# Attention probabilities transposed in 32 by 32 blocks on VectorE and moved across partitions by DMA, in place of TensorE transposes

## Chip, cores and metric

The kernel runs on one core of a Trainium2 chip. The metric is the device time of one execution in microseconds, of which the median over the timed runs counts.

## What is computed

Two transformer layers over 8 batches of 112 tokens of width 1024. Each layer is a cross attention to 375 context rows and a small mixture of low rank experts, with a layer norm ahead of each. The change touches the attention of the second layer, which the reference computes so (32 query heads in 8 groups of 4, each group with one key and value head, head width 128):

```
q = (query @ wq).reshape(bs, sq, HQ, DK).transpose(0, 2, 1, 3)
k = (key @ wk).reshape(bs, sk, HKV, DK)        # repeated for the 4 heads of a group
v = (value @ wv).reshape(bs, sk, HKV, DV)
q = apply_rope(q, pos)
k = apply_rope(k, curr_seq_pos + jnp.arange(sk))
scores = jnp.einsum('bhqd,bhkd->bhqk', q, k) / scale
attn = jax.nn.softmax(scores + m[:, None, :, :], axis=-1)
out = jnp.einsum('bhqk,bhkd->bhqd', attn, v)
return out.transpose(0, 2, 1, 3).reshape(bs, sq, HQ * DV) @ wo
```

## The kernel before

Every float32 product is made of three TensorE passes over operands that are split into a high and a low part (`split_product`, line 204: high x high, high x low, low x high). The high part is a copy on ScalarE (ACT) into a rounded type, the low part a subtraction on VectorE (DVE) or GpSimd (POOL).

The first layer, the key and value projections and the query projection (`query1_phase`) come first. The attention then runs as 64 **steps** (`attention_phase`), one for each group g of 4 heads and each batch u, with s = 8g + u. The steps are written out one by one on each engine. The order on an engine is the order of its instructions, engines wait for each other by semaphores, and all DMAs are issued from one queue, SP's. In step s:

- TensorE makes the scores of step s+1 (4 heads, 12 matmuls of 376 columns), the transposes of the probabilities of step s (line 1780, 12 of them: 4 heads by 3 tiles of 128 keys, through the identity into three PSUM banks), 24 matmuls of 448 columns, and the output of step s (9 matmuls of 448 columns: v by transposed probabilities). The 24 are the output projection of an earlier quad of batches (`project`); in the first four steps (`FILLED`) they are the last of the query projection.
- VectorE adds the mask to the scores and takes their maximum (line 1515), negates it (1519), later scales the exponentials by the inverse sum (1535), makes the low parts of the transposed probabilities (1722) and of the output (1736), and adds up the projection (1713).
- ScalarE takes the exponentials (1526), copies the high parts of the transposed probabilities out of PSUM (1659), and makes the high parts of q (1476), k (1478), v, the output and the output weights.
- GpSimd makes the low parts of q, k (both line 1491), v (1496) and the output weights (1683).
- SP loads q, k and v of later steps (lines 1460, 1463, 1468), in half of the steps a tile of output weights (1617), and in the first steps stores the last rotated queries.

The score tile `e_scores` has the queries in partitions and the keys in the row, so the probabilities must be transposed before they can meet v, whose keys are in partitions.

Of the kernel before, what the change touches and what calls it, by code (L numbers as in the profile page):

```python
# [14 lines left out]
ALU = mybir.AluOpType  # L15
# [21 lines left out]
LOWEST = -3.4028234663852886e38  # L37
# [69 lines left out]
class LoraSems:  # L107
    def __init__(self, sem, name):
        self.mid = sem(f"{name}_mid")
        self.chain = sem(f"{name}_chain")  # L110
        self.gate_exp = sem(f"{name}_gexp")
# [98 lines left out]
def build(nc, x, ctx_nat, ctx_t, mask, wq0_t, wk0, bq, bk, a0, b0, wq1, wk1, wv1, wo1, a1, b1,  # L210
# [5 lines left out]
    with ExitStack() as outer:  # L216
# [16 lines left out]
        with ExitStack() as heads, ExitStack() as layer0:  # L233
# [5 lines left out]
            with ExitStack() as context, nc.Block() as block:  # L239
# [11 lines left out]
                last_heads = query1_phase(nc, k, first, q1, layer0, block)  # L251
                layer0.close()
                attention_phase(nc, k, first, last_heads, heads, block)
# [570 lines left out]
def layer0_phase(nc, k, keys, chunks, q1, ctx, block):  # L824
# [36 lines left out]
    sn, sl = NormSems(sem, "ln23"), LoraSems(sem, "lora0")  # L861
# [349 lines left out]
def query1_phase(nc, k, first, q1, buffers, block):  # L1211
# [3 lines left out]
    sb, _, _ = buffers_of(nc, buffers)  # L1215
    sem = k.sem
    bank = k.banks[4:8]
    rope = sb("q_rope", [P, 2, SEQ])
    straight, crossed = sb("q_straight", [P, 2, HALF]), sb("q_crossed", [P, 2, HALF])
# [20 lines left out]
    def _(sp):  # L1240
# [22 lines left out]
        with sp.Fori(1, LAST - 2) as i:  # L1263
# [6 lines left out]
        load_w(LAST - 2, 0)  # L1270
        first.load(sp)
        for t in range(2):
            if t == 1:
                load_w(LAST - 2, 1)
            for h in range(2):
                store(4 * (LAST - 2) + 2 * t + h, LAST - 2, t, h)
        load_w(LAST - 1, 0)
        first.load_next(sp)
        for t in range(2):
            if t == 1:  # L1280
                load_w(LAST - 1, 1)
            for h in range(2):
                store(4 * (LAST - 1) + 2 * t + h, LAST - 1, t, h)
# [7 lines left out]
    def _(act):  # L1291
# [10 lines left out]
        with act.Fori(2, LAST - 1) as i:  # L1302
            for t in range(2):
                weight_high(i, t, 4 * i + 2 * t + 2)
        weight_high(LAST - 1, 0, 4 * LAST - 2)
        first.split_high(act)
        weight_high(LAST - 1, 1, 4 * LAST)
        weight_high(LAST, 0, 4 * LAST + 2)
        first.exps(act, 0, 0, range(PER_GROUP))
# [3 lines left out]
    def _(pool):  # L1313
# [5 lines left out]
        with pool.Fori(1, LAST - 1) as i:  # L1319
            for t in range(2):  # L1320
                weight_low(i, t)
        weight_low(LAST - 1, 0)
        first.split_low(pool)
        weight_low(LAST - 1, 1)
        weight_low(LAST, 0)
        weight_low(LAST, 1)
# [21 lines left out]
    def _(dve):  # L1348
# [7 lines left out]
        with dve.Fori(1, LAST - 1) as i:  # L1356
# [3 lines left out]
        unit = 4 * (LAST - 1)  # L1360
        first.take_mask(dve)
        rotated_half(dve, unit, LAST - 1, 0, 0)
        first.mask_scores(dve, 0, 0, (0, 1))
        rotated_half(dve, unit + 1, LAST - 1, 0, 1)
        first.mask_scores(dve, 0, 0, (2, 3))
        rotated_half(dve, unit + 2, LAST - 1, 1, 0)
        first.normalise(dve, 0, 0)
        rotated_half(dve, unit + 3, LAST - 1, 1, 1)
# [10 lines left out]
    def _(pe):  # L1379
# [12 lines left out]
        with pe.Fori(1, LAST - 1) as i:  # L1392
# [3 lines left out]
        unit = 4 * (LAST - 1)  # L1396
        half_tile(unit, LAST - 1, 0, 0)
        first.scores(pe, 0, 0, (0, 1))
        half_tile(unit + 1, LAST - 1, 0, 1)
        first.scores(pe, 0, 0, (2, 3))  # L1400
        half_tile(unit + 2, LAST - 1, 1, 0)
        half_tile(unit + 3, LAST - 1, 1, 1)
# [17 lines left out]
class AttentionSteps:  # L1420
# [5 lines left out]
    def __init__(self, nc, ctx, k):  # L1426
        sb, pair, sem = buffers_of(nc, ctx, "right")
        self.k = k
        self.s_bank = k.banks[0:2]
        H = PER_GROUP  # L1430
        self.raw_q, self.raw_k = sb("e_raw_q", [P, 2, H, SEQ]), sb("e_raw_k", [P, 2, KEYS_EVEN])
        self.raw_v = sb("e_raw_v", [P, 2, KEY_TILES, P])
        self.q, self.kt = pair("e_q", [P, 2, H, SEQ]), pair("e_k", [P, 2, KEYS_EVEN])
# [611 lines left out]
```

## Time and profile before

| | |
|---|---|
| median of 3 runs | 1875.65 us (1875.37 to 1876.58) |
| profiled execution, its own time | 1872.77 us |
| its span, first to last instruction | 1870.7 us |
| busy: PE, DVE, ACT, POOL | 98%, 58%, 34%, 33% of the span |
| mean granted TensorE clock | 0.998 of full speed |
| attention steps: first transposes of step 0 to those of step 63 | 1149.1 to 1781.5 us of the span |

The span is cut into stages with different limits, so shares over the whole say little about the attention alone. A matmul's row shows a duration that overlaps with the next one's. What one costs is the distance between starts.

### The profile page before, as it was taken

The numbers are of one execution on the slowest core, as the hardware profiler recorded it, in microseconds if no ns is written. First come the engines' busy times: TensorE is split into PE (matmuls) and PEld (weight loads), VectorE is DVE, ScalarE is ACT, GpSimd is POOL, SyncE is SP. The second block draws the span as 40 slices with busy tenths as digits, with TensorE's granted clock in tenths as the row PEclk, the third lists the DMA queues.
The fourth block names the chain that finished last, engine by engine and source line by source line (L and its number), as shares of the span: only waits on it lengthen the run. The fifth ranks groups of instructions, "written<-read, shape, count | busy, mean of one in ns | idle before, by whom it ended". The sixth has DMA issues, their size and how long they took to land.

```text
span 1870.7 us, 27823 instructions
## 1 busy us (share of the span) xinstructions
PE 1829.2 (98%) x9628; PEld 1643.6 (88%) x9628; DVE 1091.2 (58%) x2481; ACT 636.2 (34%) x1345; POOL 610.1 (33%) x427
## 2 busy tenths in 40 slices
PE   6999999999999999999999999999999999999997
PEld 5999899999777777778999999899999999999985
DVE  5631275657222222126666668877777777777766
ACT  4211210102222222222111013666656666665612
POOL 2323531226222222202222233444435444353413
PEclk9999999999999999999999999999999999999999
DMA  4112342344533333314223234332323323232223
GB/s 125 57 56 78 131 130 80 101 137 147 169 121 120 116 118 108 110 61 132 96 93 105 100 117 128 107 97 79 103 76 99 92 79 108 78 92 85 59 74 108
DMA packets 138317, 190.40 MB, mean 102 GB/s; under 512 B 42672, under 2 KB 109360, under 8 KB 137328
## 3 DMA queue, kind: packets, MB, share of 16 engines
q1 hardware_dynamic: 138224, 189.21, 32.3%
q8 instruction: 52, 0.85, 0.2%
q14 instruction: 41, 0.34, 0.1%
HBM read 142.25 MB, written 46.92 MB: 101 GB/s over the span
## 4 chain that ended last, share of the span: by engine, by line
PE 83%; DVE 3%; issue 1%; DMA 1%; POOL 1%; ACT 0%; SPq 0%; DVEq 0%; POOLq 0%; ACTq 0%
PE bank L204 74%; PE bank L1780 4%; PE bank L1167 2%; PE bank L184 1%; PE bank L197 1%; PE bank L101 1%; DVE e_scores L1535 1%; DMA aw_weights_then_ctx_rows<-in_wk 1%; DVE e_scores L1515 0%; POOL w_rest_low L756 0%; DVE e_p_t_low L1722 0%; PE bank L1152 0%; DVE e_mask_then_layer_ffn L77 0%; DVE q_rotated_then_x_rows L1929 0%; DVE e_mask_then_layer_ffn L92 0%
## 5 line engine op out<-in xcount | busy, mean ns | idle before, releaser
L204 PE MATMUL bank<-shared_operand_high,w_first_high 128*128 128x448 f32 (+1 forms) x768 | 280.2, 365 | 6.2 <-POOL w_first_low L491 2.7
L204 PE MATMUL bank<-shared_operand_low,w_first_high 128*128 128x448 f32 (+1 forms) x768 | 279.4, 364 | 0.0
L204 PE MATMUL bank<-shared_operand_high,w_first_low 128*128 128x448 f32 (+1 forms) x768 | 279.3, 364 | 0.0
L1526 ACT ACTIVATE e_scores<-e_scores,e_nmax 112x375 f32<-112x375 f32 x256 | 155.5, 615 | 120.2 <-DVE e_nmax L1519 114.7
L317 POOL TENSOR_TENSOR shared_operand_low<-ctx_raw,shared_operand_high 128x768 fp32r<-128x768 f32 x64 | 118.4, 1863 | 204.0 <-ACT shared_operand_high L313 204.0
L204 PEld LDWEIGHTS bank<-shared_operand_high,w_first_high 128*128 128x128 f32 x768 | 145.3, 189 | 18.8 <-POOL w_first_low L491 3.0
L204 PEld LDWEIGHTS bank<-shared_operand_high,w_first_low 128*128 128x128 f32 x768 | 145.2, 189 | 11.7
L204 PEld LDWEIGHTS bank<-shared_operand_low,w_first_high 128*128 128x128 f32 x768 | 145.2, 189 | 11.2
L1515 DVE CUSTOM_DVE_ANT_0 e_scores<-bank,e_mask_then_layer_ffn 112x375 f32<-112x375 f32 x256 | 139.8, 546 | 9.2 <-PE bank L1780 0.4
L1316 POOL TENSOR_TENSOR w_first_low<-aw_weights_then_ctx_rows,w_first_high 128x1024 fp32r<-128x1024 f32 x30 | 71.7, 2391 | 224.4 <-ACT w_first_high L1298 224.4
L1496 POOL TENSOR_TENSOR e_v_low<-e_raw_v,e_v_high 128x384 fp32r<-128x384 f32 x64 | 65.2, 1019 | 226.6 <-ACT e_v_high L1485 226.6
L204 PE MATMUL bank<-shared_operand_high,w_rest_high 128*128 128x376 f32 x384 | 128.8, 335 | 2.7 <-POOL w_rest_low L756 2.7
L204 PE MATMUL bank<-shared_operand_low,w_rest_high 128*128 128x376 f32 x384 | 128.6, 335 | 0.0
L204 PE MATMUL bank<-shared_operand_high,w_rest_low 128*128 128x376 f32 x384 | 128.6, 335 | 0.0
L313 ACT ACTIVATE shared_operand_high<-ctx_raw 128x768 fp32r<-128x768 f32 x64 | 52.8, 842 | 210.6 <-DMA ctx_raw<-in_ctx_t 192.4
L1713 DVE TENSOR_TENSOR y_t<-bank,y_t 128x448 f32<-128x448 f32 x112 | 70.0, 625 | 87.0 <-PE bank L204 85.3
L1298 ACT ACTIVATE w_first_high<-aw_weights_then_ctx_rows 128x1024 fp32r<-128x1024 f32 x30 | 31.8, 1061 | 253.1 <-PE bank L204 240.2
L204 PE MATMUL bank<-w_rest_high,shared_operand_high 128*128 128x512 f32 x288 | 112.9, 392 | 0.0
L204 PE MATMUL bank<-w_rest_high,shared_operand_low 128*128 128x512 f32 x288 | 112.5, 391 | 0.0
L204 PE MATMUL bank<-w_rest_low,shared_operand_high 128*128 128x512 f32 x288 | 112.2, 389 | 0.0
L1722 DVE TENSOR_TENSOR e_p_t_low<-bank,e_p_t_high 128x448 fp32r<-128x448 f32 x192 | 107.6, 616 | 5.8 <-ACT e_p_t_high L1659 5.8
L1535 DVE TENSOR_SCALAR e_scores<-e_scores,e_inv 112x375 f32<-112x375 f32 x256 | 96.9, 437 | 2.2
(243 smaller groups left out, 4404.3 us busy)
## 6 DMA issues: line engine op xcount, KB each, us to landing
ctx_raw<-in_ctx_t SPq DMA_DIRECT2D x64, 384.0 KB, 3.7
e_raw_wo<-in_wo SPq DMA_DIRECT2D x32, 512.0 KB, 4.9
aw_weights_then_ctx_rows<-in_wq SPq DMA_DIRECT2D x30, 512.0 KB, 3.5
q_rotated<-q_rotated_then_x_rows SPq DMA_DIRECT2D x64, 224.0 KB, 1.9
e_raw_q<-q_rotated SPq DMA_DIRECT2D x64, 224.0 KB, 2.8
v_rows<-v_out SPq DMA_DIRECT2D x48, 256.0 KB, 2.1
e_raw_v<-v_rows SPq DMA_DIRECT2D x64, 192.0 KB, 3.4
k_rotated<-k_rotated_sb SPq DMA_DIRECT2D x64, 188.0 KB, 1.9
```

Source lines behind the costliest of these rows:

```text
L204: mm = pe.matmul(out, stationary[a], moving[b], start=(first and i == 0), stop=(last and i == 2))
L313: act.activation(k.ctx_ring[0][slot][:, 2 * j:2 * j + 2, :], k.c_raw[:, j % 2], ACT.Copy).then_inc(done, 1)
L317: pool.tensor_tensor(k.ctx_ring[1][slot][:, 2 * j:2 * j + 2, :], k.c_raw[:, j % 2], f32(k.ctx_ring[0][slot][:, 2 * j:2 * j + 2, :]), ALU.s ...
L1167: mm = pe.matmul(row_banks[h][0:SEQ, :], et[:, kt, :], cn[:, kt, h * 512:(h + 1) * 512], start=(kt == 0), stop=(kt == KEY_TILES - 1))
L1316: pool.tensor_tensor(k.w_first[1][:, t], k.raw[:, t], f32(k.w_first[0][:, t]), ALU.subtract).then_inc(w_low, 1)
L1496: pool.tensor_tensor(self.v[1][:, t], self.raw_v[:, t], f32(self.v[0][:, t]), ALU.subtract).then_inc(self.v_low, 1)
L1515: dve.tensor_tensor_reduce(self.s_buf[:, t, h, 0:KEYS], self.s_bank[h % 2][0:SEQ, 0:KEYS], self.mask[:, u, :], 1.0, LOWEST, ALU.add, ALU.m ...
L1526: act.activation(self.s_buf[:, t, h, 0:KEYS], self.s_buf[:, t, h, 0:KEYS], ACT.Exp, bias=self.nm[:, t, h:h + 1], accum_out=self.total[:, t ...
L1535: dve.tensor_scalar(self.s_buf[:, t, h, 0:KEYS], self.s_buf[:, t, h, 0:KEYS], self.inv[:, t, h:h + 1], None, ALU.mult).then_inc(self.norme ...
L1713: dve.tensor_tensor(k.yt[:, tile, at:at + HALF], y_bank[t][:, 0:HALF], k.yt[:, tile, at:at + HALF], ALU.add).then_inc(y_added, 1)
L1722: dve.tensor_tensor(pt[1][:, c, :], p_bank[c][:, 0:HALF], f32(pt[0][:, c, :]), ALU.subtract).then_inc(pt_low, 1)
L1780: mm = pe.transpose(p_bank[c][:, h * SEQ:(h + 1) * SEQ], s_buf[:, t, h, c * P:(c + 1) * P], k.ident[0:SEQ, 0:SEQ])
```

## The change

The queries of a batch, 112, are laid out as 4 blocks of 28 in 4 times 32 partitions, the spare places being zero, so that the scores fill 128 partitions. VectorE transposes the probabilities of two heads by one instruction (32 by 32 blocks, each within its 32 partitions), twice a step. The blocks of one query block then lie in the wrong partitions for three quarters of the keys. SP issues 16 DMAs a step, from 32 partitions of one SBUF tile to 32 partitions of another, 384 floats in each, which bring them together (`shuffle`). The 12 TensorE transposes of a step and their PSUM banks are gone. So are the 4 negations: the query rotation carries a minus sign, the mask is negated once, VectorE takes the minimum, and the exponential is taken with scale -1.

Scores are made three steps ahead of their use, normalised and transposed two steps ahead. ScalarE normalises two of the four heads, GpSimd makes two of the three low parts of the probabilities, now from SBUF instead of PSUM. The scores have four banks, the output two.

```diff
     def scores(self, pe, s, u, heads):
...
-            split_product(pe, self.s_bank[h % 2][0:SEQ, 0:KEYS_EVEN], [x[:, t, h, :] for x in self.q],
+            split_product(pe, self.s_bank[h][:, 0:KEYS_EVEN],
+                          [x[:, t, h].rearrange("p i b -> p (i b)") for x in self.q],
                           [x[:, t, :] for x in self.kt], True, True).then_inc(self.scored, 1)
...
+    def normalise_last(self, act, s, u):
+        t = u % 2
+        act.wait_ge(self.inverted, s + 1)
+        for h in (2, 3):
+            act.activation(self.s_buf[:, t, h, 0:KEYS], self.s_buf[:, t, h, 0:KEYS], ACT.Copy,
+                           scale=self.inv[:, t, h:h + 1]).then_inc(self.last_normed, 1)
+
+    def transpose(self, dve, s, u, heads):
...
+        dve.transpose(self.in_blocks[:, t, :, h * piece:(h + 2) * piece].rearrange("p j (m k) -> p m j k", k=BLOCK),
+                      self.s_buf[:, t, h:h + 2, :].rearrange("p h (c j k) -> p (h c) j k", j=BLOCKS, k=BLOCK)
+                      ).then_inc(self.transposed, 1)
+
+    def shuffle(self, sp, s):
...
+        sp.wait_ge(self.transposed, 2 * s + 2)
+        if s >= 2:
+            sp.wait_ge(self.pt_low_first, s - 1)
+            sp.wait_ge(self.pt_low, 2 * s - 2)
+        for i in range(BLOCKS):
+            for j in range(BLOCKS):
+                sp.dma_start(self.pt_raw[t][BLOCK * j:BLOCK * (j + 1), i],
+                             self.in_blocks[BLOCK * i:BLOCK * (i + 1), t, j]).then_inc(self.shuffled[t], 16)
...
         def step(s, u, g):
...
-            for c in range(KEY_TILES):
-                if s >= 1:
-                    pe.wait_ge(pt_low, 3 * s - 3 + c + 1)
-                elif c == 2:
-                    pe.wait_ge(last_heads.read, last_heads.units + 1)
-                for h in range(H):
-                    mm = pe.transpose(p_bank[c][:, h * SEQ:(h + 1) * SEQ],
-                                      s_buf[:, t, h, c * P:(c + 1) * P],
-                                      k.ident[0:SEQ, 0:SEQ])
-                mm.then_inc(turned, 1)
+            if s + AHEAD < STEPS:
+                first.scores(pe, s + AHEAD, u + AHEAD, range(H))
```

On SP's queue a middle step with a tile of output weights holds these rows before (q, k, v, output weights):

```order
L1460 DMA e_raw_q<-q_rotated 128x4x112
L1463 DMA e_raw_k<-k_rotated 128x376
L1468 DMA e_raw_v<-v_rows 128x3x128
L1617 DMA e_raw_wo<-in_wo 128x4x256
L1460 DMA e_raw_q<-q_rotated 128x4x112
```

and these now, where `e_shuffled` and `e_shuffled_then_xn_t` are the two targets of the shuffle and `q_rotated_then_x_rows` holds the transposed blocks:

```order
L1639 DMA e_shuffled_then_xn_t<-q_rotated_then_x_rows 32x384 x16
L1516 DMA e_raw_then_a<-q_rotated 128x4x112
L1519 DMA e_raw_then_a<-k_rotated 128x376
L1524 DMA e_raw_then_a<-v_rows 128x3x128
L1735 DMA e_raw_wo<-in_wo 128x4x256
L1639 DMA e_shuffled<-q_rotated_then_x_rows 32x384 x16
```

Four DMAs a step became twenty; the sixteen stand behind the step's loads and ahead of the next step's.

On VectorE a middle step before, from the mask of the first head (ISA rows of line 1515 are the masking and its accumulator read):

```order
L1515 ISA e_scores,e_max<-bank,e_mask_then_layer_ffn 112x375
L1519 TENSOR_SCALAR e_nmax<-e_max 112x1
L1722 TENSOR_TENSOR e_p_t_low<-bank,e_p_t_high 128x448 x3
L1713 TENSOR_TENSOR y_t<-bank,y_t 128x448
...
L1532 RECIPROCAL e_inv<-e_total 112x4
L1535 TENSOR_SCALAR e_scores<-e_scores,e_inv 112x375 x4
L1736 TENSOR_TENSOR e_o_t_first_low<-bank,e_o_t_first_high 128x4x112
```

and a whole step now, the accumulator reads left out:

```order
L1597 RECIPROCAL e_inv<-e_total 128x4
L1603 TENSOR_SCALAR e_scores<-e_scores,e_inv 128x375
L1840 TENSOR_TENSOR e_o_t_second_low<-bank,e_o_t_second_high 128x4x4x28
L1582 ISA e_scores,e_least<-bank,e_mask_then_layer_ffn 128x375
...
L1603 TENSOR_SCALAR e_scores<-e_scores,e_inv 128x375
...
L1625 STREAM_TRANSPOSE q_rotated_then_x_rows<-e_scores 128x6x4x32
L1859 TENSOR_TENSOR e_p_t_low<-e_shuffled,e_p_t_high 128x448
...
L1625 STREAM_TRANSPOSE q_rotated_then_x_rows<-e_scores 128x6x4x32
...
L1834 TENSOR_TENSOR y_t<-bank,y_t 128x448 x2
```

Two transposes came in, spread between the masks. One low part and two scalings are left, and both additions of the projection stand at the end of the step.

## Rows read from the trace of the kernel before

**Rows 1.** The page, part 1: busy us, share of the span, instructions.

```profile
PE 1829.2 (98%) x9628; PEld 1643.6 (88%) x9628; DVE 1091.2 (58%) x2481; ACT 636.2 (34%) x1345; POOL 610.1 (33%) x427
```

**Rows 2.** The chain that ended last, 1400 to 1500 us: start, us, what.

```profile
1412.89 1.15 PE bank L1780 x12
1414.05 8.81 PE bank L204 x45
```

**Rows 3.** Busy time by stretch: us; PE, PEld, DVE, ACT, POOL; clock; DMA share; GB/s.

```profile
1149.10:1781.50 632.40, 629.04 (x3598) 589.14 (x3596) 502.42 (x1460) 394.86 (x977) 274.19 (x220) 1.00 0.32 91
1412.73:1422.70 9.97, 9.97 (x59) 9.37 (x58) 7.85 (x24) 6.66 (x17) 5.50 (x4) 1.00 0.44 117
1442.00:1452.00 10.00, 10.00 (x59) 9.41 (x58) 7.77 (x24) 5.87 (x16) 3.13 (x3) 1.00 0.22 63
```

**Rows 4.** Groups by line: out<-in, shapes, count; busy us, mean ns; idle before.

```profile
L1722 DVE TENSOR_TENSOR e_p_t_low<-bank,e_p_t_high 128x448 fp32r<-128x448 f32 x192 | 107.6, 616 | 5.8 <-ACT e_p_t_high L1659 5.8
L1491 POOL TENSOR_TENSOR e_q_low<-e_raw_q,e_q_high 128x448 fp32r<-128x448 f32 x64 | 74.9, 1170 | 56.7 <-ACT e_q_high L1476 56.7
```

**Rows 5.** Timeline of PE, then of PEld: start, us, instruction.

```profile
300.00 0.33 PE L204 MATMUL bank<-shared_operand_high,w_first_high 128*128 128x376 f32 x1
300.17 0.34 PE L204 MATMUL bank<-shared_operand_low,w_first_high 128*128 128x376 f32 x1
...
300.00 0.19 PEld L204 LDWEIGHTS bank<-shared_operand_low,w_first_high 128*128 128x128 f32 x1
```

**Rows 6.** Timeline of DVE in one step.

```profile
1450.61 1.45 DVE L1535 TENSOR_SCALAR e_scores<-e_scores,e_inv 112x375 f32<-112x375 f32 x4
...
1453.39 0.15 DVE L1519 TENSOR_SCALAR e_nmax<-e_max 112x1 f32<-112x1 f32 x1
1453.58 0.55 DVE L1515 CUSTOM_DVE_ANT_0 e_scores<-bank,e_mask_then_layer_ffn 112x375 f32<-112x375 f32 x1
...
1454.24 1.68 DVE L1722 TENSOR_TENSOR e_p_t_low<-bank,e_p_t_high 128x448 fp32r<-128x448 f32 x3
```

**Rows 7.** Timeline of ACT in one step.

```profile
1442.65 0.51 ACT L1478 ACTIVATE e_k_high<-e_raw_k 128x376 fp32r<-128x376 f32 x1
...
1444.44 0.62 ACT L1526 ACTIVATE e_scores<-e_scores,e_nmax 112x375 f32<-112x375 f32 x1
...
1445.04 0.62 ACT L1526 ACTIVATE e_scores<-e_scores,e_nmax 112x375 f32<-112x375 f32 x1
```

**Rows 8.** Timeline of SP's queue in one step: start and us of each issue.

```profile
1401.12 0.37 SPq L1468 DMA_DIRECT2D e_raw_v<-v_rows  x1
1401.54 0.55 SPq L1617 DMA_DIRECT2D e_raw_wo<-in_wo  x1
1408.02 0.37 SPq L1460 DMA_DIRECT2D e_raw_q<-q_rotated  x1
1408.43 0.51 SPq L1463 DMA_DIRECT2D e_raw_k<-k_rotated  x1
```

**Rows 9.** Timeline of SP's queue, runs of issues without a wait.

```profile
0.75 0.87 SPq L379 DMA_DIRECT2D b_x_rows<-in_x  x2
1.67 0.42 SPq L387 DMA_DIRECT2D ident<-in_ident_in  x1
...
4.02 0.90 SPq L383 DMA_DIRECT2D aw_weights_then_ctx_rows<-in_wq_t  x2
...
466.34 0.57 SPq L885 DMA_DIRECT2D c_x_rows<-in_x  x1
```

**Rows 10.** Timeline of DVE, then of POOL, in the query projection.

```profile
1083.96 0.63 DVE L1341 TENSOR_TENSOR q_rotated_then_x_rows<-q_straight,q_crossed 128x448 f32<-128x448 f32 x1
...
1088.92 2.00 DVE L1341 TENSOR_TENSOR q_rotated_then_x_rows<-q_straight,q_crossed 128x448 f32<-128x448 f32 x1
...
1088.04 2.39 POOL L1316 TENSOR_TENSOR w_first_low<-aw_weights_then_ctx_rows,w_first_high 128x1024 fp32r<-128x1024 f32 x1 [7.53 <-ACT w_first_high L1298]
```

**Rows 11.** The page, part 6: issues, count, KB each, median us to landing.

```profile
k_rotated<-k_rotated_sb SPq DMA_DIRECT2D x64, 188.0 KB, 1.9
```

More of the change, by code:

```diff
@@ L1261, in _ @@
         first.load_mask(sp)
-        with sp.Fori(1, LAST - 2) as i:
+        with sp.Fori(1, LAST - 3) as i:
             for t in range(2):
@@ L1269, in _ @@
             sp.wait_ge(s, 16 + 16 * PER_GROUP // 2)
[L1270 to L1283, printed above, removed]
+        for i in range(LAST - 3, LAST):
+            load_w(i, 0)
+            if i == LAST - 3:
+                first.load_qk(sp, 0, 0, 0)
+                first.load_qk(sp, 1, 1, 0)
+            for t in range(2):
+                if t == 1:
+                    load_w(i, 1)
+                if i == LAST - 2:
+                    first.load_qk(sp, 2 + t, 2 + t, 0)
+                for h in range(2):
+                    store(4 * i + 2 * t + h, i, t, h)
+                if i == LAST - 2 and t == 1:
+                    first.shuffle(sp, 0)
+                if i == LAST - 1:
+                    if t == 0:
+                        first.load_v(sp, 0, 0, 0)
+                        first.load_qk(sp, 4, 4, 0)
+                        first.load_v(sp, 1, 1, 0)
+                    else:
+                        first.shuffle(sp, 1)
+                        first.load_qk(sp, 5, 5, 0)
     def store_last(sp, n):
@@ L1355, in _ @@
             rotated_half(dve, unit, 0, t, h)
-        with dve.Fori(1, LAST - 1) as i:
+        first.pad(dve)
+        with dve.Fori(1, LAST - 2) as i:
             for t in range(2):
@@ L1481, in v_high_part @@
         t = u % 2
-        act.wait_ge(self.v_in[t], 16 * half_of(s, u) + 16)
-        if not (known(s) and s < 2):
+        act.wait_ge(self.v_in[t], 16 * (s // 2) + 16)
+        if s >= 2:
             act.wait_ge(self.o_acc, s - 1)
@@ new lines, in pad, with negate_mask, attention_buffers @@
+    def pad(self, dve):
+        for x in self.q:
+            dve.memset(f32(x[:, :, :, :, QUERIES:BLOCK]), 0.0).then_inc(self.padded, 1)
+        dve.memset(self.s_buf[:, :, :, KEYS:KEYS_PAD], 0.0).then_inc(self.padded, 1)
+    def negate_mask(self, act):
+        act.wait_ge(self.mask_in, 16)
+        act.activation(self.mask, self.mask, ACT.Copy, scale=-1.0).then_inc(self.padded, 1)
+    def take_mask(self, dve):
+        dve.wait_ge(self.padded, 4)
+def attention_buffers(nc, ctx, k, first):
+    sb, pair, _ = buffers_of(nc, ctx)
@@ L1636, in step @@
                 last_heads.store(sp, s - 1)
-        for q_stored in first.q_stored:
-            sp.wait_ge(q_stored, 16 + 16 * (HEADS // 2 - 1))
+            if s + 2 < STEPS:
+                first.shuffle(sp, s + 2)
         steps(sp, step)
@@ L1841, in final_phase @@
     SLOTS = X_SLOTS
-    xr, spare = first.rows[0:SEQ], first.s_buf
+    xr, spare = first.rows[0:SEQ], first.s_buf[0:SEQ]
     sb = carve(first.mask_region)
@@ L1877, in _ @@
         for b in range(SLOTS):
+            if b == 2:
+                for s in first.shuffled:
+                    sp.wait_ge(s, 256 * GROUPS * BATCH // 2)
             load(b)
```

408 lines of the change are left out of this document (240 added, 168 removed).

## Prediction

> **What bounds the kernel now.** I read the page's busy shares first: PE has work for 98% of the span, every other engine for at most 58% [rows 1]. The chain of waits says the same of the attention alone. It alternates between two rows, 1.15 us in the twelve transposes and 8.81 us in the 45 other matmuls of a step, and starts over after 9.97 us [rows 2, 3]. No other engine is on it. From the transposes of step 0 to those of step 63 it takes 632.4 us, where 63 steps of 9.97 are 628.1, so stalls hold only 4.3 us [rows 3]. Shares by stretch show what room the others have: in a step with output weights DVE is busy 7.85 us, ACT 6.66, POOL 5.50, and DMAs 0.44 of the time; without, 7.77, 5.87, 3.13 and 0.22 [rows 3]. The queue of SP is in none of these shares. Its timeline shows four issues a step, about 1.8 us [rows 8].
>
> **TensorE.** 64 times 1.16 us go (9.97 less 8.81), 74.2 us [rows 2, 3]. The scores' weights now have 128 columns instead of 112. That costs nothing: with weights of 128 columns and 376 moving ones, starts in the key projection lie 0.17 us apart although a load's row says 0.19 [rows 5]. What is left of a step is 8.81 us. The scores of steps 1 and 2 only move ahead of step 0 (2 times 12 times 0.17 = 4.1 us). If nothing else holds TensorE, 64 steps take 64 x 8.81 less three without scores (6.2), 557.7 us. From its first scores to its last output the loop before took 632.4 + 1.0 + 7.9 = 641.3 us (1.0 for six score matmuls ahead of the first transposes; 7.9 for the last step behind them: 1.15, 24 matmuls and 9 at 0.205). So the gain of this case is 641.3 - 561.8 = 79.5 us, which includes the stalls.
>
> **VectorE.** Of 7.8 us, 4 negations go (0.19 from start to start), 2 low parts (1.68 for three) and 2 scalings (1.45 for four): 5.2 us are left [rows 6]. The trace shows no VectorE transpose. Bound below by one element a cycle: a mask of 375 elements takes 0.55 us, a low part of 448 takes 0.62 [rows 4, 6], so 1 ns an element, and 768 elements 0.93 us; two make 1.9. Bound above by two passes, 1.25 us each more than a low part's, 1.8 us; two make 3.6. I take the first, as every VectorE row here follows it. That gives 7.1 us, before waits.
>
> Such waits are seen. The addition of line 1341 has two SBUF inputs and takes 0.63 us, but 2.00 us where it starts at 1088.92, inside a GpSimd instruction that ends at 1090.43: it stood still until then and ran for 0.5 [rows 10]. Now the low part of the probabilities on VectorE has two SBUF inputs too (before, one was in PSUM), and GpSimd has two more instructions of 1.17 us each step [rows 4]. I price one such wait a step at half of a GpSimd instruction to a whole one, 0.5 to 1.2 us, and up to 0.4 for the scalings. VectorE then needs 7.6 to 8.7 us of 8.81: close, not over. The Trainium skill, page "SBUF — State Buffer", section "SBUF: two separate sides", calls this an exclusive lock, held for a whole instruction, of GpSimd against VectorE's operations with two SBUF inputs or in a two-port mode; by that rule, the trace agrees, and a scaling can meet GpSimd's longest instruction too (2.4 us with output weights), which would put VectorE at some 9.9 us in half of the steps. That is a case below, not the sum.
>
> **ScalarE and GpSimd.** ScalarE gets two scalings of 375 (0.51 us at most, as k's copy [rows 7]): 7.7 us with output weights, 6.9 without. GpSimd: 5.50 + 2.34 = 7.8 and 5.5 us, if rows of 28 elements cost what whole ones do. Both fit into 8.81. The loop from ScalarE's copy of the output through VectorE's masks and back (exponential at 0.60 us [rows 7], copies) comes to some 8.1 us plus the wait: also below, on average.
>
> **SP's queue.** This is where I see the new bound. No row has a DMA of 32 partitions, so bounds: an issue after a wait takes 0.37 us and 0.04 to the next start, 0.41 [rows 8]; nine in a run, from 0.75 to 4.92 us, 0.463 each, whether 64 KB or 512 KB [rows 9]; the slow ones 0.57 and 0.05, 0.62 [rows 9]. The sixteen come in a run, so I take 0.463. The others cost 0.42 (q), 0.55 (k), 0.47 (v behind k), 0.60 (output weights) from start to start [rows 8]. A step is then 16 x 0.463 + 1.44 = 8.85 us, 9.45 with output weights, 9.15 on average: more than 8.81. In total, from the shuffle of step 1, which stands behind the last store ahead of step 0: that one and a q and k load 8.4; 62 shuffles 459.3; 58 q and k loads 56.3; 62 of v 29.1; 32 of output weights 19.2; 4 stores 1.6; sum 573.9. Then 1 us for its late start, 2 to land (1.9 for 188 KB [rows 11]), 3.5 for the copies and low parts, 1.8 for the last nine matmuls: 582. That is 24 us later than TensorE would be.
>
> The Trainium skill, page "DMA: Bandwidth & Descriptors", section "Rules for kernel authors", speaks against the change: many small transfers should be one large, and under 64 KB one pays mostly overhead. Each of the sixteen is 48 KB. Rows 9 bear that out for the issue, which costs the same at 64 KB as at 512. By the page one transfer a step would leave 1800, sixteen give the sum.
>
> The data are less of a problem: 786 KB more a step beside the 0.22 to 0.44 DMA share. By the share per byte (0.44 at 117 GB/s) 89 GB/s more add 0.33; the faster step raises the old part by 1.1. That is up to 0.8. Landing may slow, but the chain from the second transpose of step s+2 (about 7 us into step s) over 7.4 us of issues to the copies of step s+2 (1.5 us into it) leaves 19.1 - 14.4 - 2 = 2.7 us.
>
> **Sum.** 582 + 4.1 = 586.1 us against 641.3: 55 us less. From the profiled execution's 1872.8 that gives 1817.6; its own median lies 2.9 higher, so **1821 us**.
>
> **Rivals.**
> - *Issue-bound, as summed*: 1821 (1812 to 1835, for 0.45 to 0.48 an issue). For it: every run in rows 9 but the slow one. Chance 0.42.
> - *TensorE stays the bound.* If a DMA of 32 partitions is issued at 0.41 us, SP needs 8.3 us a step and is hidden. 1872.8 - 79.5 + 2.9 = 1796, and some 4 us for the first four steps, where VectorE has three products and an addition of the rotation (4 times 0.63 [rows 10]) in place of two additions to the projection (1.2) and so needs some 1 us more than TensorE: 1800. It speaks for this that the rows after many-row transfers (k after q) are the longer. Chance 0.28.
> - *VectorE becomes the bound*: two passes for the transpose, 7.6 to 8.7 plus 1.7, about 9.8 us a step: 64 x 1.0 over 1796, 1860. Or VectorE stands still for whole GpSimd instructions, at the scalings too: 8.7 us, and 9.9 with output weights, some 9.4 a step, 1796 + 64 x 0.6 = 1834. Together 0.17.
> - *Slower than before.* An SBUF to SBUF issue costs as the slow rows do, 0.62 us: 992 x 0.157 = 156 us over 1821, 1977; at k's 0.55 it is 1907. It decides from 0.52 us an issue. For it: the 0.51 to 0.57 rows, which I can't explain. Against: the run of nine, at 0.42 to 0.45 each. Chance 0.09.
> - *No gain*, two of these balancing near 1876: 0.04.
>
> Under 0.2% (about 4 us) a measurement can't tell from no change. Faster: 0.42 + 0.28 + 0.17 = 0.87; same 0.04; slower 0.09. The range takes in the TensorE case below and half of the VectorE cases above: 1797 to 1852; the likeliest case's own is 1812 to 1835.
>
> **What the profile after would show.** No rows with `ident,e_scores`; in the attention 45 matmuls a step. If right, the chain names DMA or SP between PE pieces, ScalarE's copies of the probabilities wait for the shuffle, SP's queue has no gap, steps last 9.1 to 9.2 us, shorter in the steps without output weights only late in the loop. If TensorE is the bound, steps last 8.81 and SP waits for VectorE. If VectorE is, the transpose's row is over 1.3 us, or low parts and scalings stand at over 1 us beside GpSimd's. I am wrong above all if the issue of a small SBUF to SBUF DMA isn't like the 128-partition loads, in either direction.

## The result, and the profile after

The changed kernel takes **2048.97 us** (median of four runs, 2044.52 to 2052.31) beside 1875.67 us for the kernel before (1875.37 to 1876.58) on the same chip: a ratio of 1.0922, 95% interval 1.0900 to 1.0943. It is 9% slower. The prediction was 1821 us in a range of 1797 to 1852, with a chance of 0.09 for slower. It was wrong in sign and by 228 us.

The page of the changed kernel, parts 1, 4 and 6 (busy us and share of the span; the chain that ended last, by engine and by line; issues with KB and us to landing):

```profile
PE 1826.7 (89%) x8860; PEld 1615.5 (79%) x8860; DVE 1109.5 (54%) x2099; ACT 701.0 (34%) x1474; POOL 777.1 (38%) x555
...
PE 48%; SPq 27%; DMA 5%; DVE 4%; issue 4%; POOL 2%; ACT 1%; DVEq 0%; ACTq 0%; POOLq 0%
...
e_shuffled<-q_rotated_then_x_rows SPq DMA_DIRECT2D x512, 48.0 KB, 2.0
e_raw_wo<-in_wo SPq DMA_DIRECT2D x32, 512.0 KB, 6.3
```

TensorE has 768 matmuls fewer and nearly the same busy time as in [rows 1]: it waits, and a matmul that runs at a lower clock lasts longer. SP's queue, which was not on the chain before, now holds 27% of it. Busy time by stretch, where [rows 3] had TensorE at 99 to 100% and a clock of 1.00:

```profile
1188.00:1890.00 702.00, 546.69 (x2482) 490.61 (x2480) 445.72 (x929) 392.98 (x951) 381.22 (x301) 0.88 0.49 133
```

PE is busy for 78% of it, VectorE for 63%, the DMA engines for 0.49. Nothing in this row is full. What is full shows in the timeline of SP's queue (start, us, instruction), to be held against [rows 8, 9]:

```profile
1402.60 10.51 SPq L1639 DMA_DIRECT2D e_shuffled_then_xn_t<-q_rotated_then_x_rows  x16
1413.16 0.58 SPq L1516 DMA_DIRECT2D e_raw_then_a<-q_rotated  x1
1413.78 0.51 SPq L1519 DMA_DIRECT2D e_raw_then_a<-k_rotated  x1
...
1416.78 10.76 SPq L1639 DMA_DIRECT2D e_shuffled<-q_rotated_then_x_rows  x16
```

The chain of waits over the same stretch shows both of the things that set a step, first a load of output weights and what hangs on it, then the shuffle's issues:

```profile
1401.87 7.22 DMA e_raw_wo<-in_wo
...
1409.12 1.06 ACT e_wo_third_high L1767
1410.18 0.44 ACT e_o_t_first_high L1772
...
1411.73 1.09 DVE e_scores L1603
...
1415.86 0.90 DVE q_rotated_then_x_rows L1625
...
1416.78 0.53 SPq L1639
1417.31 0.04 issue
1417.35 0.59 SPq L1639
1417.94 0.04 issue
1417.98 0.59 SPq L1639
...
1419.25 1.31 SPq L1639
```

From start to start a shuffle issue costs 0.63 us (1417.35 to 1417.98), not the 0.463 of the sum. Sixteen are 10.1 us, more than the 8.81 that TensorE needs for everything in a step. (Each of the two runs of sixteen above lasts some 0.5 us longer, because a single issue in it is slow, as the one of 1.31 us here.) The issues of q, k and v add 0.63, 0.55 and 0.47, so a step is at least 11.8 us, and 12.5 with output weights. To see what steps really last, I take SP's issue of v. It comes once a step. The first two of the 64 stand ahead of the loop; these are the third and the last:

```profile
1171.08 0.43 SPq L1524 DMA_DIRECT2D e_raw_then_a<-v_rows  x1
...
1947.34 0.58 SPq L1524 DMA_DIRECT2D e_raw_then_a<-v_rows  x1
```

From the third to the last there are 61 intervals, so 776.3 / 61 = **12.73 us a step**. The issues at their usual prices (the medians in this trace) give 12.1. The other 0.63 us fall into two parts. In 0.32 us a step (19.5 us in all) the queue stands between two issues. Another 0.31 us a step comes from 25 of the 1188 issues, which last 0.8 to 1.7 us each. Of these, 22 fall together with the 22 packets of 16 KB that the DMA queue `q8 instruction` moves in this stretch, and mostly end 0.35 to 0.39 us after such a packet:

```profile
q8 instruction: 46, 0.75, 0.2%
```

This row is from the page's part 3 (packets, MB, share of 16 engines; here over the whole span). In each of the six traces with twelve or sixteen transfers a step, all 22 such packets fall into a slow issue. So SP seems to stop for the fetch of its own program, written out issue by issue; no run varied this. The step is worked out in the same way for each experiment below.

### The profile page after: what moved, and what is told of

It is laid out like the page before. It is cut to its first block, busy times and chain, and to the rows that moved or that the text cites. A ratio compares the mean times of both kernels' runs of the same rounds, so it can differ in the third digit from the quotient of the medians.

```text
span 2050.3 us, 27030 instructions
## 1 busy us (share of the span) xinstructions
PE 1826.7 (89%) x8860; PEld 1615.5 (79%) x8860; DVE 1109.5 (54%) x2099; ACT 701.0 (34%) x1474; POOL 777.1 (38%) x555
## 4 chain that ended last, share of the span: by engine, by line
PE 48%; SPq 27%; DMA 5%; DVE 4%; issue 4%; POOL 2%; ACT 1%; DVEq 0%; ACTq 0%; POOLq 0%
PE bank L206 43%; SPq L1639 23%; DMA e_raw_wo<-in_wo 4%; PE bank L1171 2%; SPq L1516 1%; SPq L1519 1%; PE bank L186 1%; SPq L1524 1%; PE bank L199 1%; PE bank L103 1%; DVE e_p_t_low L1859 1%; DVE q_rotated_then_x_rows L1625 1%; DVE e_scores L1603 1%; DVE e_scores L1582 1%; DMA aw_weights_then_ctx_rows<-in_wk 0%
## 5 line engine op out<-in xcount | busy, mean ns | idle before, releaser
L206 PE MATMUL bank<-e_p_t_high,e_v_high 128*128 128x448 f32 x192 | 87.7, 457 | 157.5 <-DVE e_p_t_low L1859 153.6
L206 PEld LDWEIGHTS bank<-e_p_t_high,e_v_high 128*128 128x128 f32 x192 | 42.2, 220 | 183.4 <-issue 166.6
L1590 ACT ACTIVATE e_scores<-e_scores,e_least 128x375 f32<-128x375 f32 x256 | 153.1, 599 | 61.7 <-DVE e_least L1582 61.7
L1625 DVE STREAM_TRANSPOSE q_rotated_then_x_rows<-e_scores 128x768 f32<-128x768 f32 x128 | 124.2, 971 | 60.2 <-issue 59.9
L206 PEld LDWEIGHTS bank<-shared_operand_high,w_first_low 128*128 128x128 f32 x768 | 145.1, 189 | 12.1
L1582 DVE CUSTOM_DVE_ANT_0 e_scores<-bank,e_mask_then_layer_ffn 128x375 f32<-128x375 f32 x256 | 134.7, 529 | 0.0
L1603 DVE TENSOR_SCALAR e_scores<-e_scores,e_inv 128x375 f32<-128x375 f32 x128 | 117.2, 917 | 2.3
L1840 DVE TENSOR_TENSOR e_o_t_first_low<-bank,e_o_t_first_high 128x448 fp32r<-128x448 f32 x32 | 20.0, 624 | 177.6 <-ACT e_o_t_first_high L1772 177.4
```

Of the source, the lines that this page charges most:

```text
L206: mm = pe.matmul(out, stationary[a], moving[b], start=(first and i == 0), stop=(last and i == 2))
L1582: dve.tensor_tensor_reduce(self.s_buf[:, t, h, 0:KEYS], self.s_bank[h][:, 0:KEYS], self.mask[:, u, :], 1.0, HIGHEST, ALU.add, ALU.min, sel ...
L1590: act.activation(self.s_buf[:, t, h, 0:KEYS], self.s_buf[:, t, h, 0:KEYS], ACT.Exp, bias=self.least[:, t, h:h + 1], scale=-1.0, accum_out= ...
L1603: dve.tensor_scalar(self.s_buf[:, t, h, 0:KEYS], self.s_buf[:, t, h, 0:KEYS], self.inv[:, t, h:h + 1], None, ALU.mult).then_inc(self.norme ...
L1625: dve.transpose(self.in_blocks[:, t, :, h * piece:(h + 2) * piece].rearrange("p j (m k) -> p m j k", k=BLOCK), self.s_buf[:, t, h:h + 2, : ...
```

## Experiments

The three kernels that carry blocks through DRAM were run four times each. Every other kernel of this section was run once. Runs of one and the same kernel lie up to 8 us apart, so a difference of about 10 us between single runs is not clear of noise.

**What an issue costs by its form.** Nine runs of transfers behind the end of the kernel before, each run waited for before the next begins (`settle`).

```diff
+                for n in range(12):
+                    sp.dma_start(b[32 * (n % 4):32 * (n % 4) + 32, n // 4], a[32:64, n // 4]).then_inc(done, 16)
+                settle(12)
+                for n in range(4):
+                    sp.dma_start(b[:, n], a[:, n]).then_inc(done, 16)
+                settle(4)
...
```

> The kernel before, with a block behind its end in which SP issues runs of DMAs of ten forms, each run waited for before the next: 12 of 32 partitions by 384 floats SBUF to SBUF (the form of the change), 4 of 128 by 384, 8 of 64 by 384 and 12 of 128 by 96 SBUF to SBUF, 12 of 32 by 384 to DRAM, 12 of 32 by 384 and 4 of 128 by 384 from DRAM, 12 of 32 by 96 SBUF to SBUF, 4 of 32 by 4 by 384 from DRAM. The changed kernel shows 0.634 us an issue. If the cost hangs on both sides being SBUF, every such form costs about 0.6, and the forms with DRAM 0.46. If it hangs on 32 partitions, all forms of 32 cost about 0.6, those of 64 less, those of 128 0.46. If it hangs on bytes, the form of 32 by 96 is much cheaper than that of 32 by 384.

Timeline of SP's queue there (start, us of the whole run, number of issues; `form_a` and `form_b` are in SBUF, `form_d` and `form_e` in DRAM):

```profile
1881.98 7.58 SPq L282 DMA_DIRECT2D form_b<-form_a  x12
1890.94 2.48 SPq L285 DMA_DIRECT2D form_b<-form_a  x4
...
1901.74 7.56 SPq L291 DMA_DIRECT2D form_b<-form_a  x12
1910.61 5.42 SPq L294 DMA_DIRECT2D form_d<-form_a  x12
1917.27 5.62 SPq L297 DMA_DIRECT2D form_b<-form_e  x12
...
1929.30 7.53 SPq L303 DMA_DIRECT2D form_b<-form_a  x12
```

From start to start, an issue from SBUF to SBUF costs 0.63 us whether it has 32 partitions x 384 floats (line 282), 128 x 384 (285), 128 x 96 (291) or 32 x 96 (303). With DRAM on one side it costs 0.455 (store, 294) and 0.47 (load, 297), and 0.45 in a run of loads of 128 x 384. So among these forms the price goes neither with partitions nor with bytes, but with where the two ends are. That is not the whole rule: the loads of k and of the output weights, and the slow rows of [rows 9], have a DRAM end too and cost 0.55, 0.66 and 0.62 from start to start. Why they do was not tested. Every issue in [rows 8, 9] has a DRAM end. The trace of before has no SBUF to SBUF transfer at all.

**Four wide transfers instead of sixteen** carry the same bytes, each block straight across without the exchange; the exchange is left out of the result.

```diff
-            for j in range(BLOCKS):
-                sp.dma_start(self.pt_raw[t][BLOCK * j:BLOCK * (j + 1), i],
-                             self.in_blocks[BLOCK * i:BLOCK * (i + 1), t, j]).then_inc(self.shuffled[t], 16)
+            sp.dma_start(self.pt_raw[t][:, i], self.in_blocks[:, t, i]).then_inc(self.shuffled[t], 16)
```

> The changed kernel with the sixteen DMAs of a shuffle replaced by four of 128 partitions by 384 floats each: the same bytes a step, but no block leaves its 32 partitions, so this leaves out the exchange between partitions. Theory 1, the queue of SP issues too slowly: 12 issues a step go, 7.6 us, SP then needs some 4 us a step and TensorE is the bound again: 1796 to 1820. Rival, the bytes (DMA share 0.5) or their landing hold it: still above 1980. Rival, VectorE standing still behind GpSimd in low parts and scalings: VectorE's rows at 1 to 1.3 us stay, steps of 9.5 us or more, 1840 to 1900.

It took 1808.7 us. Steps last 8.79 us. Busy time by stretch:

```profile
1300.00:1700.00 400.00, 399.08 (x2036) 373.09 (x2035) 344.17 (x769) 324.83 (x788) 314.75 (x247) 1.00 0.60 189
```

TensorE is full, and its clock is back at 1.00. So all engine work of the change, transposes, scalings and low parts on the new engines, fits under TensorE's 8.8 us. The slowdown does not come from this work, nor from the number of bytes. What is left is that there are sixteen transfers, or that they cross partitions.

**Sixteen and twelve transfers within partitions**, SBUF to SBUF, same bytes, nothing exchanged: is it the number, or the crossing of partitions?

```diff
-            for j in range(BLOCKS):
-                sp.dma_start(self.pt_raw[t][BLOCK * j:BLOCK * (j + 1), i],
-                             self.in_blocks[BLOCK * i:BLOCK * (i + 1), t, j]).then_inc(self.shuffled[t], 16)
+            for m in range(4):
+                sp.dma_start(self.pt_raw[t][:, i, 96 * m:96 * (m + 1)],
+                             self.in_blocks[:, t, i, 96 * m:96 * (m + 1)]).then_inc(self.shuffled[t], 16)
```

> Sixteen transfers a step of 128 partitions x 96 floats, each from a partition of in_blocks to the same partition of pt_raw, in place of the sixteen of 32 x 384: the same number of issues and the same bytes, SBUF on both sides, but nothing crosses partitions (the exchange of the blocks is left out, so the output is not the reference's). Theory (the number of issues from SBUF to SBUF sets the time, 0.63 us each, whatever their form): the time of the changed kernel, 2035 to 2060 us, with sixteen issues 0.634 us apart on SP's queue. Rival (crossing partitions, or the 32-partition form, is what costs): near the kernel with four wide transfers a step, 1809 to 1850 us.

> Twelve transfers a step of 128 partitions x 128 floats, again within partitions (the exchange is left out), the same bytes. Theory: the time goes with the number of issues. A step of SP's queue is then 12 x 0.634 + 1.64 = 9.25 us, 9.95 with output weights, on average 9.6 us over the 62 steps, above TensorE's need of about 8.8, so 1845 to 1875 us. Rival (what sets the time is not the issues but the landing of the bytes or the order of the waits): within 30 us of the changed kernel, 2020 to 2050 us.

Sixteen: 2043.0 us, 12.58 us a step, as the changed kernel. Crossing partitions costs nothing that shows. Twelve: 1920.6 us, 10.64 us a step. The number decides, as expected, but the size was missed (1845 to 1875 us): issues alone give 9.6 to 9.7 us. Of the other us, single slow issues make 0.28, and for 0.73 the queue waits. The next two experiments take up why.

**Sixteen transfers with a DRAM source.** Everything stays, count, bytes, destination and waits, but the source is a block of the output weights (the probabilities are left out of the result).

```diff
-                             self.in_blocks[BLOCK * i:BLOCK * (i + 1), t, j]).then_inc(self.shuffled[t], 16)
+                             self.k.wo1[0, BLOCK * i:BLOCK * (i + 1), j, 0:384]).then_inc(self.shuffled[t], 16)
```

> The changed kernel with one thing other: each of the sixteen transfers of 32 x 384 floats reads a block of the output weights in DRAM in place of the transposed probabilities in SBUF. Count, bytes, destination and every wait stay as they are (the probabilities are thereby left out of the output). Theory (what the prediction had wrong is the price of an issue with SBUF on both sides, 0.634 us, and not the number of issues): with 0.45 to 0.47 us an issue the step of SP's queue is 16 x 0.465 + 1.5 = 8.9 us, 9.6 with output weights, and the time 1815 to 1860 us, which is where the prediction stood. Rival (sixteen transfers a step cost as much whatever their source): 2020 to 2060 us.

Timeline of SP's queue:

```profile
1409.30 7.39 SPq L1639 DMA_DIRECT2D e_shuffled<-in_wo  x16
1416.74 0.43 SPq L1516 DMA_DIRECT2D e_raw_then_a<-q_rotated  x1
...
1428.69 0.56 SPq L1735 DMA_DIRECT2D e_raw_wo<-in_wo  x1
1432.86 7.29 SPq L1639 DMA_DIRECT2D e_shuffled<-in_wo  x16
```

The issues cost what the prediction took: 7.39 / 16 = 0.46 each, and q only 0.47 behind them. The shortest steps without output weights last 8.98 us. Yet the whole took **1912.7 us**, at 10.56 us a step: not 1821, and outside the 1815 to 1860 that I expected of this run. So 92 of the 228 us were not the price. The gap from 1429.25 to 1432.86 shows what: SP's queue waits. Its cause is on ScalarE and VectorE, whose timelines over the same stretch read (in brackets the idle time before, and what ended it):

```profile
1425.20 1.06 ACT L1767 ACTIVATE e_wo_first_high<-e_raw_wo 128x1024 fp32r<-128x1024 f32 x1 [9.06 <-DMA e_raw_wo<-in_wo]
...
1426.58 1.10 ACT L1610 ACTIVATE e_scores<-e_scores,e_inv 128x375 f32<-128x375 f32 x2
...
1426.72 0.63 DVE L1840 TENSOR_TENSOR e_o_t_first_low<-bank,e_o_t_first_high 128x448 fp32r<-128x448 f32 x1 [9.25 <-ACT e_o_t_first_high L1772]
...
1431.87 0.97 DVE L1625 STREAM_TRANSPOSE q_rotated_then_x_rows<-e_scores 128x768 f32<-128x768 f32 x1
```

The tile of output weights is asked for at 1418.99, behind the sixteen issues of the shuffle before, and lands 6.2 us later. ScalarE waits for it in its order ahead of its scalings, VectorE waits for ScalarE and makes its transposes only behind that, and the next shuffle (1432.86) waits for the second transpose, which ends at 1432.84. Behind that shuffle stand the loads of the next step, another tile of weights among them. This is a loop: queue, landing, ScalarE, VectorE, queue.

**Output weights one step earlier**, in that kernel and in the changed kernel itself:

```diff
-            if g > 0 and u < 4:
-                load_wo(u, g)
+            if u == 7 and g + 1 < GROUPS:
+                load_wo(0, g + 1)
+            if g > 0 and u < 3:
+                load_wo(u + 1, g)
```

> The kernel with sixteen transfers a step from the weights in DRAM (it leaves the probabilities out as that one does), with the tiles of output weights asked for one step earlier. That kernel took 1912.7 us although its steps without output weights are the 9.0 us of issues that the prediction took; its steps with output weights take 10 to 14 us. Theory (the second term that the prediction left out is the closed chain of waits in the steps with output weights: the tile issued behind sixteen transfers, ScalarE waiting for it ahead of its scalings, VectorE and SP's queue behind those): with the tile early those steps fall to 10 or 11 us and the time to 1840 to 1875 us. Rival (the long steps come from the engines' work and its order, not from the tile's landing): 1895 to 1915 us.

> The changed kernel with each tile of output weights loaded one step earlier, for the groups after the first. Steps with such a tile last 13.1 us on average against 11.8 in the others, where the longer queue of SP explains 12.5. Theory: the tile lands 7 us after its issue, ScalarE stands before it (95 us in all before the first tile's copy), its scalings come late, then VectorE's transposes, and SP has to wait before the shuffle. The tile in time, steps with weights fall to 12.5: some 20 us less than the changed kernel, 2025 to 2035. Rival, the excess comes from something else (VectorE against GpSimd): no change, 2045 to 2052.

With a DRAM source 1867.7 us (45 less; 9.79 us a step, against 9.34 of issues alone), as the theory had it. In the changed kernel 2038.3 us, only 11 less and outside the 2025 to 2035 that I expected, at 12.49 a step. By the medians these 11 us are hardly more than noise, but the traces show the same: over the 61 steps the time in which SP's queue stands still falls from 57.5 to 3.2 us with the DRAM source, and from 19.5 to 3.1 in the changed kernel. The more the issues themselves take, the less a late tile adds.

**The exchange through DRAM.** One store of the blocks of a step, and four loads that gather them, each with a DRAM end. Nothing is left out.

```diff
+        sp.dma_start(self.k.blocks_dram[t], self.in_blocks[:, t]).then_inc(self.blocks_out[t], 16)
+
+    def fetch(self, sp, s):
...
+        for j in range(BLOCKS):
+            sp.dma_start(self.pt_raw[t][BLOCK * j:BLOCK * (j + 1)],
+                         self.k.blocks_dram[t, :, j].rearrange("(i k) x -> k i x", k=BLOCK)
+                         ).then_inc(self.shuffled[t], 16)
```

> The changed kernel with the shuffle through DRAM: one store of the transposed blocks of a step (128 partitions by 6 KB), and one step of the queue later four loads of 32 partitions by 4 by 384 floats, which bring the same blocks to the same places. Five issues instead of sixteen, but twice the bytes and a second landing. Theory 1 (issues are the bound): SP needs 5 x 0.5 to 0.63 plus 1.7, at most 4.9 us a step; the blocks are in place 6 us into the step before they are needed; TensorE is the bound, 1800 to 1830, faster than the kernel before. Rival, the DMA engines become the bound (share 0.5 of 12 us a step now, and 786 KB more): above 10 us a step, 1880 or more.

> The kernel that carries the blocks through DRAM (one store and four loads a step), with the tiles of output weights asked for one step earlier. Theory (its last waits of note are those of ScalarE for late output weights): 1809 to 1820 us, and the chain of waits loses its share of e_raw_wo. Rival (the transfer engines, busy 0.98 of the stretch, hand the wait on to another transfer): 1820 to 1826 us.

It took 1823.2 us, ratio to before 0.9724 (0.9707 to 0.9741), and with the weights asked for one step earlier **1809.1 us**, ratio 0.9669 (0.9653 to 0.9685): faster than both kernels, by 3.3% and 11.7%. (Like for like the way through DRAM takes 226 us less than the direct one with late weights, 1823 against 2049, and 229 less with early ones, 1809 against 2038.) Busy time by stretch of the second:

```profile
1300.00:1700.00 400.00, 399.33 (x2036) 372.98 (x2034) 359.59 (x764) 324.51 (x785) 313.89 (x247) 1.00 0.99 276
```

TensorE is full again, though the DMA engines are as well (0.99). Their load is hidden: the store lands 5.8 us after its issue and the loads 4.5, but the blocks are asked for a step of the queue ahead.

**A quarter of the blocks straight, the rest through DRAM**: four SBUF to SBUF issues more, to relieve the DMA engines.

```diff
         for j in range(BLOCKS):
+            sp.dma_start(self.pt_raw[t][BLOCK * j:BLOCK * (j + 1), 0],
+                         self.in_blocks[0:BLOCK, t, j]).then_inc(self.shuffled[t], 16)
-            sp.dma_start(self.pt_raw[t][BLOCK * j:BLOCK * (j + 1)],
-                         self.k.blocks_dram[t, :, j].rearrange("(i k) x -> k i x", k=BLOCK)
+            sp.dma_start(self.pt_raw[t][BLOCK * j:BLOCK * (j + 1), 1:BLOCKS],
+                         self.k.blocks_dram[t, BLOCK:P, j].rearrange("(i k) x -> k i x", k=BLOCK)
                          ).then_inc(self.shuffled[t], 16)
```

> As the kernel before it in this list, but the first block of query rows goes straight from SBUF to SBUF in four transfers and only the other three blocks go through DRAM (one store, four loads). SP's queue has about 4 x 0.634 + 5 x 0.46 + 1.6 = 6.4 us of issues a step, under TensorE's 8.8, and a quarter fewer of the bytes pass through DRAM. Theory (the transfer engines' load is what still costs): 1809 to 1818 us and a DMA share clearly below 0.98. Rival (the number of transfers loads the engines, not the way): no faster than with all blocks through DRAM, 1820 to 1830 us.

It took 1857.6 us (ratio to before 0.9922, 0.9906 to 0.9939), 48 more than with all blocks through DRAM, and neither theory had that. The DMA share did fall, to 0.83. The chain of waits:

```profile
1399.48 4.49 DMA p_blocks<-q_rotated_then_x_rows
...
1403.99 0.53 SPq L1651
...
1404.56 0.58 SPq L1653
...
1408.77 5.57 DMA p_blocks<-q_rotated_then_x_rows
```

The queue waits until a store has landed (4.5 and 5.6 us), then issues eight transfers (4.7 us), and only behind them the next store. That closes a loop of some 9.6 us (9.61 a step), above TensorE's 8.8, while the queue's issues add up to about 7. With four loads in place of eight transfers the same loop is 5.8 + 1.9 = 7.7 us, below 8.8, which fits the kernel before this one; no run varied the order. I had counted issues, and not what they stand in front of.

**Forms in alternation**, to see whether a change of form costs:

```diff
+                for pair in ((inside, load), (inside, store), (load, store), (inside, half), (load, tall)):
+                    for n in range(12):
+                        pair[n % 2](n)
+                    settle(12)
```

> The kernel before with five runs of twelve transfers behind its end, each run alternating two forms of 32 x 384 floats: SBUF to SBUF with a load from DRAM, SBUF to SBUF with a store to DRAM, a load with a store, SBUF to SBUF with one of half the columns, and a load of 32 partitions with one of 128 partitions x 32 columns. Theory (an issue costs what its own form costs): pairs of 1.09 us in the first two runs, 0.92 in the third, 1.27 in the fourth and 0.91 in the fifth. Rival (a change of form from one issue to the next costs by itself): pairs of 1.15 to 1.2 us in the first two, as where the two kinds alternated in the kernel with part of the blocks through DRAM, and the others too above the sums of their forms. The time as a whole is that of before plus about 50 us.

Timeline of SP's queue, SBUF to SBUF (line 282) with a load (285), then the load with a store (288):

```profile
1885.02 0.51 SPq L282 DMA_DIRECT2D form_b<-form_a  x1
1885.58 0.58 SPq L285 DMA_DIRECT2D form_b<-form_e  x1
1886.20 0.51 SPq L282 DMA_DIRECT2D form_b<-form_a  x1
...
1900.12 0.42 SPq L285 DMA_DIRECT2D form_b<-form_e  x1
1900.59 0.42 SPq L288 DMA_DIRECT2D form_d<-form_a  x1
```

A pair of the first kind takes 1.18 us where the forms by themselves add up to 1.10; the pair with a store in place of the load takes 1.18 too, against 1.09. The other pairs cost their sum (0.93 here, 1.27 and 0.94 in the last two). So the rival holds in part: only where a transfer within SBUF alternates with one that has a DRAM end does it cost 0.08 more a pair. And what follows a transfer within SBUF is recorded as slow: the load at 0.58 instead of 0.42. This explains q's 0.58 behind the shuffle, where [rows 8] show 0.37.

## Why the prediction was wrong

**The step that failed** is in "SP's queue": "The sixteen come in a run, so I take 0.463." That the queue would become the bound was right, and so was the form of the sum. The price was not: 0.634 us. The prediction had the case among its rivals ("An SBUF to SBUF issue costs as the slow rows do, 0.62 us", 1977 us), and its last sentence named this as the weak point, yet it gave it 0.09. It took the value from the run of nine in [rows 9] because those come in a run like the sixteen; but all nine have a DRAM end. The point from which it decides, 0.52 us, was lower still in truth: at 0.46 the kernel takes 1912.7 us and is already slower than before. Two slips in the sum are small beside this. The run in [rows 9] starts seven issues in 3.27 us, 0.467 each and not 0.463, some 4 us in all; and the case's own range for 0.45 to 0.48 us is 1808 to 1838 by its own sum, not 1812 to 1835.

**The second failure** is in the same step: the sum let the queue's issues follow each other without a gap, but for the landing at the end. The prediction had looked at one margin, that of the shuffle ("leaves ... 2.7 us"), and not at the tile of output weights, which lands later behind a busy queue and holds up ScalarE ahead of its scalings. A smaller term stood at nothing as well, the single slow issues, 0.3 to 0.36 us a step. Even with 0.634 us an issue the sum gives 1991 us, 58 short of the measured time.

The 228 us, from kernel to kernel:

| | us | step |
|---|---|---|
| predicted | 1821 | 9.15 |
| DRAM source, early weights: a step's issues 0.2 us more than in the sum, single slow issues 0.36, the queue's waits 0.05; 8 us lie outside the 61 steps | +47 = 1868 | 9.79 |
| SBUF source (with early weights) | +171 = 2038 | 12.49 |
| weights as in the change | +11 = 2049 | 12.73 |

The order matters: with a DRAM source the late weights are worth 45 us. For the row of the SBUF source the price gives 992 issues x 0.171 = 170 us, and 170.6 were measured. The closeness is partly luck. In the two traces the 61 steps take 762.0 and 596.9 us, 165 apart. From start to start a shuffle issue takes 0.653 and 0.494 us there, the slow ones included, which makes 155 of them, and q's slower issue 7 more. These are single runs on different chips, where the kernel before took 1874.7 and 1878.9 us.

Point by point:

- *TensorE, 8.81 us a step and 1800 if nothing else holds it.* Right: 8.79 a step with four transfers, and 1808.7 and 1809.1 us in the two kernels where TensorE is full. Why it is 9 us more than 1800 was not traced; the first 51 us from 1149 on hold 4 us of idle TensorE in the kernel with four transfers, where the kernel before has 1.2.
- *VectorE's transpose at 0.93 us.* Right: 0.97, and the upper bound of 1.8 was not needed. The groups by line of the changed kernel:

```profile
L1625 DVE STREAM_TRANSPOSE q_rotated_then_x_rows<-e_scores 128x768 f32<-128x768 f32 x128 | 124.2, 971 | 60.2 <-issue 59.9 <-DVE e_scores L1603 0.3
L1603 DVE TENSOR_SCALAR e_scores<-e_scores,e_inv 128x375 f32<-128x375 f32 x128 | 117.2, 917 | 2.3
L1802 POOL TENSOR_TENSOR e_p_t_low<-e_shuffled_then_xn_t,e_p_t_high 128x448 fp32r<-128x448 f32 x64 | 79.6, 1264 | 78.1 <-ACT e_p_t_high L1782 78.1
...
L1859 DVE TENSOR_TENSOR e_p_t_low<-e_shuffled,e_p_t_high 128x448 fp32r<-128x448 f32 x32 | 32.2, 1005 | 5.8 <-ACT e_p_t_high L1782 5.8
```

- *VectorE standing still beside GpSimd, 0.5 to 1.2 us for a low part and up to 0.4 for the scalings.* The low part takes 1.0 us against 0.62 in [rows 4], so 0.4. A scaling takes 0.92 where four took 1.45 in [rows 6], some 0.55 more each, two a step, so 1.1 in all. The total of 1.5 is what was priced at most; its parts were the wrong way round. It did not bound: VectorE is busy for 90% of the stretch in the fastest kernel. The case at 9.9 us a step, which followed the Trainium skill's page "SBUF — State Buffer", section "SBUF: two separate sides", did not come about, though the longer rows bear its mechanism out: of the 128 scalings 92 last over 0.7 us, and every one of these ends 0.21 us after the end of a GpSimd instruction. Of the 33 scalings of 0.5 us or less 28 meet none. The longest lasts 2.36 us, about as long as GpSimd's longest instruction:

```profile
L1603 DVE TENSOR_SCALAR e_scores<-e_scores,e_inv x128: 402/1060/2357, 1124.2 to 1940.0; 128x375 f32<-128x375 f32 x128
```

This is a view of one line: shortest, median and longest in ns, then first and last start.

- *ScalarE and GpSimd fit.* Right: 81% and 78% busy in the fastest kernel. GpSimd's low parts take 1.26 us against the 1.17 taken.
- *The data are less of a problem; landing 2 us.* Right: 2.0 us, DMA share 0.49.
- *Many small transfers against one large.* The Trainium skill's page "DMA: Bandwidth & Descriptors", section "Rules for kernel authors", spoke against the change, and the runs bear out its direction: sixteen 2043, twelve 1921, four 1809 us for the same bytes. The measured reason is the issuing queue, 0.63 us an issue at any size tried, and not the transfer itself.

That the chain would name SP and that its queue would have no gap was listed as the sign of the likeliest case. It came nearly so (the gaps are 0.32 us a step), only with steps of 12.7 us where 9.1 to 9.2 were expected. The steps without output weights are shorter (12.3 us on average against 13.1, and 11.8 at the least but for the last step), and not only late in the loop.

## What to carry to other kernels

Price an issue by its own kind of transfer: where the trace has no row of that kind, the nearest rows are a guess, and the chance given to a higher price has to own up to that. When an issuing queue is near its limit, list everything that stands behind it and who waits for that; a load of weights moved by one step was worth 45 us in one kernel, 14 in the one through DRAM and 11 in the changed one, for the same edit. In this kernel a store and gathering loads through DRAM, five issues a step instead of sixteen, beat the direct way (1809 against 2038 us, both with early weights) in spite of passing twice over DMA engines that are then full. Whether sixteen direct transfers shared between two issuing queues would do as well was not tried.

## What the runs showed of the hardware

- An issue on SP's queue costs 0.63 us with both ends in SBUF, from 32 x 96 to 128 x 384 floats, and 0.45 to 0.47 with one in DRAM, in the forms tried behind the kernel's end and for q. The loads of k (0.55) and of output weights (0.66) cost more. Alternating the two kinds adds 0.08 a pair.
- Some fifty issues apart, one issue of SP takes 0.8 to 1.9 us, each time that 16 KB of instructions are fetched: 22 times in the 61 steps. All slow issues together make 0.23 to 0.36 us a step.
- VectorE's transpose of 128 x 768 floats in 32 by 32 blocks takes 0.97 us.
- DMA engines at a share of 0.99 and 276 GB/s did not slow a loop whose loads were asked for early.
- The granted clock was 1.00 where TensorE was busy throughout, and 0.88 over the stretch where it was busy for 78%; in one step of the changed kernel, of 14.4 us, 0.76, which lies between its two levels of 1.2 and 2.4 GHz (the clock is the third number from the end). Behind 5.4 us in which TensorE waited, its matmuls start 0.37 us apart; later in the same step, 0.20 apart:

```profile
1414.32:1428.75 14.43, 12.46 (x49) 11.39 (x50) 11.57 (x22) 9.19 (x22) 10.82 (x9) 0.76 0.51 135
```

```profile
1415.55 0.71 PE L206 MATMUL bank<-e_p_t_high,e_v_high 128*128 128x448 f32 x1 [5.44 <-DVE e_p_t_low L1859]
...
1416.43 0.57 PE L206 MATMUL bank<-e_p_t_high,e_v_low 128*128 128x448 f32 x1
1416.80 0.57 PE L206 MATMUL bank<-e_p_t_high,e_v_high 128*128 128x448 f32 x1
...
1424.98 0.37 PE L206 MATMUL bank<-e_o_t_first_high,e_wo_first_high 128*128 128x448 f32 x1
1425.19 0.37 PE L206 MATMUL bank<-e_o_t_first_low,e_wo_first_high 128*128 128x448 f32 x1
```

A kernel that makes TensorE wait thus also gets slower matmuls, which makes its busy share look better than its work.
